# Taking 24 transposes that nobody reads out of TensorE's beginning

## The reference

```python
latents = layernorm(x)
ln = layernorm(latents)*g + b ; xn = layernorm(ctx)*g' + b'
q = ln @ Wq.T
k, v = concat([xn @ Wkv.T, ln @ Wlkv.T])      # 77 + 512 keys, 2 heads of 64
attn = softmax(masked(rmsnorm(q)*SCALE @ rmsnorm(k).T))
x = x + (attn @ v) @ Wo.T + bo
gates = softmax(l2 @ Wg + bg)                 # l2 = layernorm(x), 8 experts
x = x + sum over the top 2 of gate * (l2 @ W[e] + b[e])
```

## Time and profile before

| what | value |
|---|---|
| median of three executions | 109.7 us |
| the profiled execution's own time | 109.68 us |
| its span, first to last instruction | 107.9 us |
| TensorE matmuls: busy, share of the span, instructions | 100.8 us, 93%, 687 |
| TensorE weight loads | 69.9 us, 65%, 687 |
| ScalarE (ACT) | 84.4 us, 78%, 198 |
| GpSimd (POOL) | 81.6 us, 76%, 85 |
| VectorE (DVE) | 69.9 us, 65%, 324 |

### The profile page before, as it was taken

One profiled execution on the slowest core, in us unless ns is written; L12 is line 12 of the kernel. 1 busy time (PEld: TensorE's weight loads), 2 busy tenths in 40 slices (PEclk: granted clock), 3 DMA queues, 4 the chain that ended last, 5 costly groups with the idle time before them and its releaser, 6 DMA issues. The chain is left out here.

```text
span 107.9 us, 2374 instructions
## 1 busy us (share of the span) xinstructions
PE 100.8 (93%) x687; PEld 69.9 (65%) x687; DVE 69.9 (65%) x324; ACT 84.4 (78%) x198; POOL 81.6 (76%) x85
## 2 busy tenths in 40 slices
PE   2999999999999999999999999999999989999950
PEld 2978877753537842897843668346888867868730
DVE  0658889732131769944461792992598989979950
ACT  0479888999698997897998299969989929697910
POOL 4337799979999197864996229988729698999990
PEclk9999999999999999999999999999999999999999
DMA  3734875000000000000000000000000001101113
GB/s 79 215 79 130 241 192 71 10 0 3 0 0 8 0 0 0 0 0 6 3 0 0 0 9 0 0 0 0 9 0 0 18 31 49 52 0 55 49 49 97
DMA packets 6823, 3.92 MB, mean 36 GB/s; under 512 B 2330, under 2 KB 6426, under 8 KB 6811
## 3 DMA queue, kind: packets, MB, share of 16 engines
q1 hardware_dynamic: 5979, 3.41, 11.8%
q10 hardware_dynamic: 832, 0.36, 1.2%
HBM read 2.72 MB, written 1.05 MB: 35 GB/s over the span
## 5 line engine op out<-in xcount | busy, mean ns | idle before, releaser
L627 ACT ACTIVATE probs<-PS,shift,rk 128x512 f32<-128x512 f32 x32 | 22.3, 786 | 2.7 <-PE PS L1110 2.6
L685 ACT ACTIVATE scaled<-PS,w 128x128 f32<-128x128 f32 x64 | 17.5, 390 | 2.4 <-POOL low L479 1.6
L1131 PE MATMUL PS<-probs,V_sb 128*64 128x512 f32 x64 | 15.3, 603 | 0.1
L977 PE MATMUL PS<-WeH,l2H 128*128 128x512 f32 x32 | 13.2, 413 | 0.4 <-issue 0.3
L979 PE MATMUL PS<-WeH,l2L 128*128 128x512 f32 x32 | 12.5, 391 | 0.0
L978 PE MATMUL PS<-WeL,l2H 128*128 128x512 f32 x32 | 12.5, 391 | 0.0
L435 POOL TENSOR_TENSOR e<-probs,probs 128x1024 f32<-128x1024 f32 x4 | 9.5, 2374 | 3.2 <-ACT probs L627 3.2
L478 POOL TENSOR_TENSOR pair<-scaled 128x512 f32<-128x512 f32 x7 | 9.0, 1288 | 3.4 <-ACT scaled L685 2.8
L426 POOL TENSOR_TENSOR esum<-probs,probs 128x1024 f32<-128x1024 f32 x4 | 9.5, 2370 | 0.6 <-ACT probs L627 0.6
L401 POOL TENSOR_TENSOR rq<-msq,half 128x8 f32<-128x8 f32 (+1 forms) x5 | 6.9, 1387 | 2.9 <-DVE msq L779 2.9
L1131 PEld LDWEIGHTS PS<-probs,V_sb 128*64 128x64 f32 x64 | 4.0, 136 | 7.7 <-issue 6.7
(11 more groups left out here) (161 smaller groups left out, 258.3 us busy)
## 6 DMA issues: line engine op xcount, KB each, us to landing
out_dram<-x SPq DMA_DIRECT2D x7, 128.0 KB, 1.7
x_sb<-in_x_dram SPq DMA_DIRECT2D x3, 256.0 KB, 4.1
We_sb<-in_L_ffn_W_dram SPq DMA_DIRECT2D x1, 512.0 KB, 5.5
We_end<-in_L_ffn_W_dram SPq DMA_DIRECT2D x1, 512.0 KB, 9.3
x_sb<-in_x_dram SPq DMA_DIRECT2D x2, 128.0 KB, 2.5
Wlkv_sb<-in_L_xattn_Wlkv_dram ACTq DMA_DIRECT2D x1, 128.0 KB, 3.0
out_dram<-x SPq DMA_DIRECT2D x2, 64.0 KB, 1.7
ctx_sb<-in_ctx_dram SPq DMA_DIRECT2D x1, 115.5 KB
```

Source lines behind the costliest of these rows:

```text
L627: act.activation(probs[p % 2][n][:, h, s], ps[:, s], ACT.Exp, bias=shift[:, 0:1], scale=rk[:, b, n, h:h + 1]).then_inc(probs_made, 1)
L685: last = act.activation(scaled[m // 2 % 2][:, m % 2, e], ps[:, e], ACT.Copy, scale=w[:, m, e:e + 1])
L977: pe.matmul(dst, lH, rH, start=True, stop=False)
L1131: last = pe.matmul(bank("value", p, 0)[h * D:(h + 1) * D, s], v, pr, start=(n == 0), stop=(n == KT - 1))
```

## The change

The four `warm` jobs are taken out of TENSOR, and with them the function `warm_`, its entry in RELEASED and the exception for it in `free`. The order of all other jobs, and their banks, stay as they are; the text of TENSOR is wrapped anew. The other engines' texts are not touched.

```diff
 TENSOR = """
-    warm 0 14 7   weights 0 0 0   warm 1 2 7   weights2 0 0 1   warm 2 4 7   xT 0 0 2   warm 3 4 7   k 0 0 3
-    v 0 0 4   xT 1 0 5   q 0 0 6   ssk 0 0 7   k 1 0 0   ctxT 0 0 1   q 1 0 2   ssk 1 0 5   v 1 0 4   ctx_v 0 0 1
...
+    weights 0 0 0   weights2 0 0 1   xT 0 0 2   k 0 0 3   v 0 0 4   xT 1 0 5   q 0 0 6   ssk 0 0 7   k 1 0 0
+    ctxT 0 0 1   q 1 0 2   ssk 1 0 5   v 1 0 4   ctx_v 0 0 1   ctx_k 0 0 7   maskT 0 0 5   xT 2 0 3   qT 0 0 0
...
         RELEASED = {
-            "warm": lambda p, n: None,
...
                 for was, wp, wn in before[kind, p, n]:
-                    if was != "warm":
-                        pe.wait_ge(*RELEASED[was](wp, wn))
+                    pe.wait_ge(*RELEASED[was](wp, wn))
...
-            def warm_(p, n):
-
-                free("warm", p, n)
-                pe.wait_ge(ident_made, 1)
-                for _ in range(n):
-                    pe.transpose(bank("warm", p, n)[:, 0:P], ident[:], ident[:])
```

More of the change, by code:

```diff
@@ L27 @@
 TENSOR = """
-    warm 0 14 7   weights 0 0 0   warm 1 2 7   weights2 0 0 1   warm 2 4 7   xT 0 0 2   warm 3 4 7   k 0 0 3
-    v 0 0 4   xT 1 0 5   q 0 0 6   ssk 0 0 7   k 1 0 0   ctxT 0 0 1   q 1 0 2   ssk 1 0 5   v 1 0 4   ctx_v 0 0 1
-    ctx_k 0 0 7   maskT 0 0 5   xT 2 0 3   qT 0 0 0   ctx_ss 0 0 6   qT 1 0 5   v 2 0 2   q 2 0 3   k 2 0 7
-    score 0 0 14   score 0 1 06   ssk 2 0 2   score 0 2 51   score 0 3 47   value 0 0 2   qT 2 0 0   value 0 1 -
-    value 0 2 -   value 0 3 -   score 0 4 63   score 1 0 15   score 1 1 47   xT 3 0 0   value 0 4 -   value 1 0 3
@@ L33 @@
[L33 to L42, removed]
@@ L43 @@
-    high 2 1 1   high 2 2 3   high 2 3 7   low 3 2 2   low 3 3 4   high 3 0 5   high 3 1 0   high 3 2 1
-    high 3 3 6   sum 3 0 2   sum 3 1 -
+    weights 0 0 0   weights2 0 0 1   xT 0 0 2   k 0 0 3   v 0 0 4   xT 1 0 5   q 0 0 6   ssk 0 0 7   k 1 0 0
+    ctxT 0 0 1   q 1 0 2   ssk 1 0 5   v 1 0 4   ctx_v 0 0 1   ctx_k 0 0 7   maskT 0 0 5   xT 2 0 3   qT 0 0 0
+    ctx_ss 0 0 6   qT 1 0 5   v 2 0 2   q 2 0 3   k 2 0 7   score 0 0 14   score 0 1 06   ssk 2 0 2
+    score 0 2 51   score 0 3 47   value 0 0 2   qT 2 0 0   value 0 1 -   value 0 2 -   value 0 3 -   score 0 4 63
@@ new lines @@
+    score 1 0 15   score 1 1 47   xT 3 0 0   value 0 4 -   value 1 0 3   den 0 0 6   score 1 2 15   proj 0 0 47
+    score 1 3 20   v 3 0 6   q 3 0 1   k 3 0 5   denT 0 0 0   score 1 4 26   value 1 1 -   value 1 2 -
+    value 1 3 -   value 1 4 -   xT 4 0 2   ssk 3 0 6   qT 3 0 0   k 4 0 4   v 4 0 7   q 4 0 3   l2T 0 0 1
+    ssk 4 0 2   den 1 0 5   score 2 0 64   score 2 1 07   score 2 2 21   gate 0 0 5   qT 4 0 4   denT 1 0 6
+    value 2 0 3   score 2 3 07   score 2 4 12   value 2 1 -   value 2 2 -   value 2 3 -   value 2 4 -
@@ new lines @@
+    proj 1 0 40   score 3 0 71   score 3 1 25   den 2 0 3   score 3 2 17   score 3 3 04   score 3 4 62
+    proj 2 0 53   denT 2 0 1   value 3 0 7   value 3 1 -   value 3 2 -   value 3 3 -   value 3 4 -   l2T 1 0 0
+    low 0 0 4   low 0 1 2   gate 1 0 6   den 3 0 1   proj 3 0 35   denT 3 0 7   low 0 2 0   low 0 3 4   l2T 2 0 2
+    low 1 0 1   low 1 1 0   low 1 2 3   high 0 0 5   high 0 1 7   high 0 2 4   high 0 3 6   high 1 0 1
+    high 1 1 0   high 1 2 3   gate 2 0 5   high 1 3 7   l2T 3 0 2   low 1 3 4   low 2 0 6   gate 3 0 2
@@ L45 @@
+    low 2 1 0   low 2 2 1   low 2 3 4   low 3 0 5   low 3 1 6   high 2 0 0   high 2 1 1   high 2 2 3   high 2 3 7
+    low 3 2 2   low 3 3 4   high 3 0 5   high 3 1 0   high 3 2 1   high 3 3 6   sum 3 0 2   sum 3 1 -
 """
@@ L1216, in sum_ @@
                     last.then_inc(sum_done, 1)
-            does = dict(sum=sum_, warm=warm_, weights=weights_, weights2=weights2_, maskT=maskT_, xT=xT_, q=q_, k=k_, v=v_, ssk=ssk_, qT=qT_,
+            does = dict(sum=sum_, weights=weights_, weights2=weights2_, maskT=maskT_, xT=xT_, q=q_, k=k_, v=v_, ssk=ssk_, qT=qT_,
                         ctxT=ctxT_, ctx_k=ctx_k_, ctx_v=ctx_v_, ctx_ss=ctx_ss_, score=score_, value=value_, den=den_, denT=denT_, proj=proj_,
```

## The result

Four executions of the changed kernel took 110.8, 111.47, 116.55 and 116.94 us, against 109.4 to 109.74 for the kernel before. The ratio is 1.0135 with a 95% interval from 1.0099 to 1.0172. The profiled execution took 110.80 us with a span of 109.0, so it is 1.12 us longer than the profiled one before, and its span 1.1 us.

The account below looks back on a forecast made before the run. The prediction took TensorE to bound the kernel from the first projection until shortly before the end. Its terms, +0.06 for the start, +1.47 for the slow clock and -0.2 absorbed, gave +1.3 us: 111.0 us, range 109.8 to 112.3.

Parts of the forecast that it names:

- What bounds the kernel: TensorE bounds from the first projection at 8.40 us until shortly before the end; 1 us lost there costs about 1 us.
- The weights come earlier: At the start, the weights' transposes begin at 4.17 instead of 4.97 us, 0.8 us earlier; WT's copy moves to 5.2.
- What takes that gain away: Before the first projection, Wo's load and the slow clock lose the 0.8 us; the projection starts at 8.46: +0.06 us.
- The clock: First projections run at half speed from 8.46 us until the rise at 12.0: +1.47 us, the main term.
- The term of 0.3 us: TensorE's waits between 8.40 and 12.70 us, which slower work fills; 0.3 us deducted from the clock's delay.
- How much reaches the end: After 12.7 us, small waits for ScalarE and VectorE absorb 0.2 us of the delay, bounds nothing and 0.5.
- The rise independent of the idle transposes: Rival at the start: clock rises at 5.7 us anyway, first projection about 0.27 us earlier, 109.4 us; chance 0.08.
- The covered delay: Rival for 8 to 28 us: ScalarE's and VectorE's timetable absorbs most of TensorE's delay, 109.8 to 110.3 us; chance 0.05.
- broken work counts too: Rival at the start: clock rises at 8 to 9.8 us despite a 0.9 us pause, 109.7 to 110.1 us; chance 0.15.
- The late rise: Rival: pauses at 5.2 and 7.6 delay the rise to 12.7 to 15.5 us, giving 111.6 to 113.0 us; chance 0.17.

Follow-up runs that it names:

- the six of the experiment: The changed kernel timed again without any edit: three executions at 111.11 to 111.23 us, three at 116.27 to 118.16.
- the fourteen late transposes: The kernel before with 14 more idle transposes ahead of ctx_v, in the fast clock: 110.91 to 111.36 us, ratio 1.0141.
- the traced execution with the pause: The changed kernel with v of piece 0 waiting until ScalarE has read k: 112.55 to 119.28 us, the traced execution 118.01.
- the ten in the gaps: The kernel before without the 14 idle transposes ahead of the weights, only the ten in gaps left: 109.53 to 111.1 us, ratio 1.0062.

## Why the prediction was right

I gave 111.0 us in a range from 109.8 to 112.3; the profiled execution took 110.80, and 0.0135 x 109.71 = 1.48 us on 109.7 makes 111.2. That is right for the shorter half of the executions. With the six of the experiment, ten executions of the changed kernel were timed; five took 110.8 to 111.5, five 116.3 to 118.2, and the median of all ten is 113.9, above my range. Nothing in the prediction says which of the two an execution will be, so it was luck that the profiled one is of the shorter group. By its own steps:

*What bounds the kernel.* Right. TensorE bounds it from the first projection on: 1.14 us at ctx_v are 1.12 us at its last piece of the chain, and the fourteen late transposes came out whole.

*The weights come earlier.* Right: 4.27 for 4.17, and the copy of WT at 5.21 for 5.2.

*What takes that gain away.* Wrong. I let weights2 start at 6.31 and lnT at 7.84, and had k at 8.46; it started at 7.86. Wo landed at 5.86 in this execution, 0.45 us earlier than in the one before, and I had taken one landing as fixed. In the ten traces read here weights2 began between 5.55 and 6.31. Of the gain of about 0.8 us that I had written off, 0.54 is real when Wo is early. An even earlier Wo adds little: in the second trace of the changed kernel weights2 began at 5.55, and k at 7.80, because xT then waits for the normalized piece.

*The clock.* Right in kind, and in length for the two traced executions: the slow stretch lasts from 7.86 to about 11.5, 3.6 us, where I took 3.54 on the analogy with the unbroken work of the start. The analogy is no rule: in the traced execution with the pause the stretch was 18 us. It cost more than I had: from k to ctx_v 13.92 - 7.86 = 6.06 us, against 12.78 - 8.40 = 4.38 before, so 1.68 us and not 1.47. The term of 0.3 us, waits that slower work fills, was too large: half of 3.64 us is 1.82, so 0.14 was filled. One idle stretch of the weight loads, 0.19 us before the second sum of squares, is still there in the changed kernel, at 13.03.

*How much reaches the end.* I took off 0.2 us; only 0.02 was to take off, 1.14 against 1.12. The sum by the measured terms is -0.54 + 1.68 - 0 = +1.14, against +0.06 + 1.47 - 0.2 = +1.33. Errors of 0.6 us, in the start of k, and of 0.4 us, in the two terms behind it, went against each other; that the sum is right to 0.2 us is partly luck.

*The rivals.* The rise independent of the idle transposes is refuted: it is at 11.5 in both traces without them, at 9.4 with ten, between 5 and 6 with the full set. With it goes, for this kernel, the statement of the Trainium skill ("TensorE: Matmul & The Clock Gate", Part 4) that transposes don't bring the full clock. The covered delay is refuted by the fourteen late transposes. That broken work counts too has the wrong time for the changed kernel, 109.7 to 110.1; with the ten in the gaps the rise comes across a pause of 0.20 us, and across one of 1.10 it isn't shown. The late rise is the rival that I sized worst. I gave it 0.17 and 111.6 to 113.0 us. If the long executions are late rises, which the trace with the pause makes likely, they are five of ten, at 116.3 to 118.2. What I missed is how late it can be: I let it come at 15.5 at the latest, and in the traced case the busy work from 12.8 to 22.6 us brought none, and it came at 26. The same page of the Trainium skill, Part 1, counts the ramp as under 1% of a typical span. The profiled execution is 1.12 us longer, 1.0%, although its slow stretch alone costs 1.68 us, 1.5%; the long executions are 6 to 8% longer.

## What to carry to other kernels

Work that nobody reads can be what brings TensorE's clock up early, and its value is the time that the real work behind it would take in the slow clock, passed on whole if TensorE bounds the rest. Size it by comparing durations of one instruction on both sides of the rise, and time such a change over many executions, since one profile shows a single moment of the rise. Idle work for the clock costs nothing where it fits into pauses that exist anyway: fourteen transposes in front of the weights held these up by 0.7 us (4.97 against 4.27), and 22 with only nine there took 0.2 to 0.4% less than the 24. With 23, eight of them in front of weights2, there was no gain, so the placing has to be timed as well.

## What the runs showed of the hardware that I had not expected

The time of the changed kernel falls into two groups 5 to 7 us apart, while the kernel before took 109.2 to 110.3 us, but for three executions named in the section on the result. In the traced slow case the clock stayed at the low level through 18 us in which TensorE worked nearly without a break behind one pause of 1.47 us, 7.86 to 26.1 us: its weight loads show two more pauses, of 0.82 and 0.22 us, and its matmuls only one, of 0.78. It may fall back after a rise: with pauses of about 1 us behind the rise, four executions of twelve had a mean granted clock of 0.977 or 0.978 and took 1.2 to 1.5 us longer. None of them was traced. The load of Wo took 3.3 to 4.1 us from issue to landing among otherwise equal starts. The granted clock of the page reads full speed before the rise in all of these profiles.
